# Attention on TensorE: products in groups of 32 output rows, a merged add on GpSimd, and an own end for the last head pair

## The reference

```python
x = x + conv_attention(group_norm(x))        # x: (16, 192, 32, 32) float32, 32 groups
# for each of the 16 images, N = 1024 pixels, 6 heads of 32 channels:
qkv  = xhat.T @ qkv_w.T                       # (N, 576)
attn = softmax(q @ k.T * 32**-0.5)            # (6, N, N)
out  = (attn @ v).reshape(N, 192) @ proj_w.T + proj_b
```

## Time and profile before

| | us |
|---|---|
| median of 3 runs | 1589.49 (1588.39 to 1589.64) |
| the profiled execution | 1588.74 |
| its span, first to last instruction | 1586.9 |
| TensorE busy | 1494.0 (94%), 8800 passes and 8800 weight loads |
| GpSimd busy | 1318.7 (83%) |
| ScalarE busy | 1197.4 (75%) |
| VectorE busy | 1165.1 (73%) |

### The profile page before, as it was taken

The page is one execution under the profiler, slowest core; times in us unless marked ns, Lnnn a source line. Parts: engine busy times, 40 slices in busy tenths (PEclk is TensorE's granted clock), DMA queues, the critical chain, the costliest instruction groups (busy, mean ns, idle before and its releaser), DMA issues.

```text
span 1586.9 us, 24547 instructions
## 1 busy us (share of the span) xinstructions
PE 1494.0 (94%) x8800; PEld 515.2 (32%) x8800; DVE 1165.1 (73%) x2022; ACT 1197.4 (75%) x2001; POOL 1318.7 (83%) x645
## 2 busy tenths in 40 slices
PE   3799999999999999999999999999999999999972
PEld 1233333333333333333333333333333333333220
DVE  4887877887787788778778877877887787877600
ACT  2277887978788797878879787887978787776850
POOL 4168988989899898989989898998989898888980
PEclk9799999999999999999999999999999999999995
DMA  3422161604325161522526152252515033241112
GB/s 102 80 38 65 42 108 36 120 23 104 58 61 108 50 105 37 100 49 65 104 54 104 44 93 45 71 99 54 108 42 93 17 82 61 55 83 39 35 48 60
DMA packets 86106, 108.87 MB, mean 69 GB/s; under 512 B 38240, under 2 KB 50912, under 8 KB 85984
## 3 DMA queue, kind: packets, MB, share of 16 engines
q1 hardware_dynamic: 85984, 107.30, 32.5%
HBM read 42.98 MB, written 13.15 MB: 35 GB/s over the span
## 4 chain that ended last, share of the span: by engine, by line
PE 68%; ACT 9%; DMA 8%; POOL 5%; SPq 4%; DVE 3%; issue 3%; POOLq 0%; DVEq 0%; ACTq 0%
PE heads_ps L615 17%; PE max_ps L524 16%; PE scores_ps L600 15%; PE extra_ps L574 6%; DMA sums_spread<-sums_sb 6%; ACT probs L729 5%; PE extra_ps L583 3%; POOL prob_pairs L793 3%; SPq L416 2%; PE extra_ps L587 2%; PE extra_ps L588 2%; PE extra_ps L585 2%; PE extra_ps L584 2%; POOL prob_pairs L799 1%; ACT xhat_a_hi L692 1%
## 5 line engine op out<-in xcount | busy, mean ns | idle before, releaser
L892 DVE TENSOR_REDUCE half_max<-max_ps 128x1 f32<-128x512 f32 x1536 | 984.3, 684 | 283.2 <-PE max_ps L524 272.8
L729 ACT ACTIVATE probs<-scores_ps,exp_scale 128x512 f32<-128x512 f32 x1536 | 974.7, 698 | 283.8 <-PE scores_ps L600 273.7
L793 POOL TENSOR_TENSOR prob_pairs<-probs 128x1024 f32<-128x1024 f32 x384 | 896.1, 2358 | 164.6 <-ACT probs L729 164.0
L524 PE MATMUL max_ps<-k_stack,q_stack 96*128 96x512 f16 x1536 | 588.7, 384 | 9.6 <-DVE half_max L892 4.8
L600 PE MATMUL scores_ps<-q_stack,k_stack 98*128 98x512 f16 x1536 | 582.5, 381 | 9.3 <-ACT probs L729 7.5
L615 PE MATMUL heads_ps<-probs,v_sb 128*32 128x512 f32 x3072 | 410.0, 606 | 1.7 <-ACT probs L729 0.8
L524 PEld LDWEIGHTS max_ps<-k_stack,q_stack 96*128 96x128 f16 x1536 | 150.4, 98 | 279.9 <-issue 105.9
L799 POOL TENSOR_TENSOR prob_pairs<-prob_pairs 128x1024 f32<-128x1024 f32 x96 | 224.1, 2355 | 0.0
L600 PEld LDWEIGHTS scores_ps<-q_stack,k_stack 98*128 98x128 f16 x1536 | 150.3, 98 | 180.1 <-ACT probs L729 39.6
L574 PE MATMUL extra_ps<-prob_pairs,ones 128*32 128x512 f32 x1152 | 134.3, 599 | 5.8 <-POOL prob_pairs L793 5.8
L615 PEld LDWEIGHTS heads_ps<-probs,v_sb 128*32 128x32 f32 x3072 | 61.0, 108 | 151.7 <-issue 130.2
(11 more groups left out here) (118 smaller groups left out, 926.1 us busy)
## 6 DMA issues: line engine op xcount, KB each, us to landing
q_stack<-qk_hi SPq DMA_DIRECT2D x96, 128.0 KB, 4.2
k_stack<-qk_hi SPq DMA_DIRECT2D x96, 128.0 KB, 5.7
inv_sb<-inv_rows SPq DMA_DIRECT2D x48, 256.0 KB
x_res<-x SPq DMA_DIRECT2D x16, 768.0 KB, 5.4
out<-x_res SPq DMA_DIRECT2D x16, 768.0 KB, 4.9
x_sb<-x SPq DMA_DIRECT2D x16, 512.0 KB, 6.6
x_sb<-x SPq DMA_DIRECT2D x32, 256.0 KB, 7.9
q_stack<-qk_lo SPq DMA_DIRECT2D x48, 128.0 KB, 4.4
```

What stands on the lines that cost most here:

```text
L524: pe.matmul(max_ps[:, bank, :], q_stack[0:STACK, par, h, P * tile:P * (tile + 1)], k_stack[0:STACK, par, h, HALF * half:HALF * (half + 1)] ...
L729: nc.scalar.activation(probs[:, a, s % RING, HALF * half:HALF * (half + 1)], scores_ps[:, u_bank(s, u), :], ACT.Exp, scale=exp_scale[:, 0: ...
L793: nc.gpsimd.tensor_tensor(prob_pairs[:, a, q, :], probs[:, a, (s - 1) % RING, :], probs[:, a, s % RING, :], ALU.add).then_inc(pairs_added, 1)
L892: nc.vector.tensor_reduce(half_max[:, a, tile, half:half + 1], max_ps[:, bank, :], AX_X, ALU.max).then_inc(max_read[bank], 1)
```

## The change

Every f16 product in the loop is issued in groups of 32 output rows, each with its own weight load of 32 columns and its own strip of 32 partitions in PSUM, so that it has the form that the weighing and the sums have. The four (or three) groups stream the same moving operand. GpSimd's adds take both heads of a pair in one operation of 2 x 1024 columns. The sums' 24 passes are split over units 2 and 3. The last pair of the last batch leaves the shared path: GpSimd stops after its first sum of four, TensorE sums the last four slots straight from `probs`, VectorE takes the reciprocal over 512 columns in PSUM and divides, the projections go to seven free banks with the third pair's part read from where it lies, and four stores replace one.

```diff
-ADDED = (2, 4, 8, 10)
-READY = (2, 6, 8, 10)
+ADDED = (1, 2, 4, 5)
+READY = (1, 3, 4, 5)
@@ tensor
+            def in_groups(to, weights, moving, start, stop):
+                for at in range(0, weights.shape[-1], D):
+                    last = pe.matmul(to[at:at + D, :], weights[:, at:at + D], moving, start=start, stop=stop)
+                return last
...
-                pe.matmul(max_ps[:, bank, :], q_stack[0:STACK, par, h, P * tile:P * (tile + 1)],
+                in_groups(max_ps[:, bank, :], q_stack[0:STACK, par, h, P * tile:P * (tile + 1)],
                           k_stack[0:STACK, par, h, HALF * half:HALF * (half + 1)],
-                          start=True, stop=True).then_inc(max_filled[bank], 1)
+                          True, True).then_inc(max_filled[bank], 1)
...
-                elif kind == "sums" and part == 0:
-                    pe.wait_ge(pairs_added, READY[-1] * (PAIRS * st.summed(i) + i + 1))
-                    for q in range(QUAD_AT, PAIRS_A_HEAD):
+                elif kind == "sums":
+                    if part == 0:
+                        pe.wait_ge(pairs_added, READY[-1] * (PAIRS * st.summed(i) + i + 1))
+                    for q in ((QUAD_AT,), range(QUAD_AT + 1, PAIRS_A_HEAD))[part]:
...
-            run_steps(step)
+            extras = run_steps(step)
+            pe.wait_ge(extra_freed, extras)
+            pe.wait_ge(pairs_added, READY[-1] * LAST + READY[QUAD_AT])
+            for n in range(RING + 1):
+                for half in range(HALVES):
+                    for a in range(2):
+                        at, cols = D * (2 * half + a), slice(HALF * half, HALF * (half + 1))
+                        summed = prob_pairs[:, a, QUAD_AT, cols] if n == 0 else probs[:, a, n - 1, cols]
+                        last = pe.matmul(extra_ps[at:at + D, :], ones[:, 0:D], summed, start=(n == 0), stop=(n == RING))
+            last.then_inc(extra_filled, 1)
...
+            pe.wait_ge(attn_moved, MOVE * ATTN_MOVES * LAST)
+            for i in range(QUARTERS):
+                product(0, last_bank(i), wp_hi[:, :, o], wp_lo[:, :, o], attn_a_hi[:, n], attn_a_lo[:, n], None)
+            pe.wait_ge(heads_hi_ready, LAST + 1)
+            pe.wait_ge(heads_lo_ready, LAST + 1)
+            for i in range(QUARTERS):
+                pe.matmul(last_bank(i), wp_hi[rows, 1, o], heads_hi[rows, :], start=False, stop=False)
+                pe.matmul(last_bank(i), wp_lo[rows, 1, o], heads_hi[rows, :], start=False, stop=False)
+                pe.matmul(last_bank(i), wp_hi[rows, 1, o], heads_lo[rows, :], start=False,
+                          stop=True).then_inc(last_projected, 1)
@@ gpsimd
-                        for a in range(2):
-                            pool.wait_ge(probs_ready, SCORE_UNITS * (SLOTS * st.b + s) + 2 * (a + 1))
-                            nc.gpsimd.tensor_tensor(prob_pairs[:, a, q, :],
-                                                    probs[:, a, (s - 1) % RING, :],
-                                                    probs[:, a, s % RING, :], ALU.add).then_inc(pairs_added, 1)
+                        pool.wait_ge(probs_ready, SCORE_UNITS * (SLOTS * st.b + s + 1))
+                        nc.gpsimd.tensor_tensor(prob_pairs[:, :, q, :], probs[:, :, (s - 1) % RING, :],
+                                                probs[:, :, s % RING, :], ALU.add).then_inc(pairs_added, 1)
...
@@ vector
+            nc.vector.reciprocal(inv_sb[:, :], extra_ps[:, :]).then_inc(inverted, 1)
+            nc.vector.tensor_tensor(heads_out[:, :], heads_ps[:, :], inv_sb[:, :], ALU.mult).then_inc(divided, 1)
+            nc.vector.tensor_tensor(heads_lo[:, :], heads_out[:, :], heads_hi[:, :],
+                                    ALU.subtract).then_inc(heads_lo_ready, 1)
```

More of the change, by code:

```diff
@@ L115 @@
 ATTN_MOVES = 4
+LAST = PAIRS * BATCH - 1
+QUARTERS = 4
 STACK_MOVES = 6
@@ L186, in due @@
             return [(self.b, self.parity, at // every)]
-        if at % every == 0 and -SLOTS <= at < 0 and self.tail:
+        if at % every == 0 and -SLOTS <= at < 0 and self.tail and not (self.closing and at == -every):
             return [(self.b - 1, 1 - self.parity, (at + SLOTS) // every)]
@@ L205, in run_steps @@
         extras = st.ordinal(SLOTS)
+    return extras
 def due(count):
@@ L491, in step @@
                         load_x(b + 4)
-                    if s == SLOTS - 1 and st.tail:
+                    if s == SLOTS - 1 and st.tail and not st.closing:
                         sp.wait_ge(extra_freed, st.ordinal(PROJ_SLOTS[-1]) + 1)
@@ L497, in _ @@
             run_steps(step)
-            sp.wait_ge(y_stored, MOVE * (BATCH + 1))
+            for i in range(QUARTERS):
+                t, half = divmod(i, 2)
+                n = slice(HALF * half, HALF * (half + 1))
+                sp.wait_ge(y_ready, i + 1)
+                sp.dma_start(out[BATCH - 1, OM * t:OM * (t + 1), n], x_res[:, t, n]).then_inc(y_stored, MOVE)
+            sp.wait_ge(y_stored, MOVE * (BATCH + QUARTERS))
         @block.tensor
@@ L552, in fill @@
                     to = extra_ps[:, C * part:C * (part + 1)]
[L553 to L557, removed]
+                    in_groups(to, xhat_a_hi[:, par, n], w_hi[:, 0, o], True, False)
+                    in_groups(to, xhat_a_hi[:, par, n], w_lo[:, 0, o], False, False)
+                    in_groups(to, xhat_a_lo[:, par, n], w_hi[:, 0, o], False, False)
+                    in_groups(to, xhat_b[:, par, n], w_hi[:, 1, o], False, False)
+                    second = in_groups(to, xhat_b[:, par, n], w_lo[:, 1, o], False, True)
                     last = second if part == 1 else None
@@ L576, in fill @@
                                                  start=(q == QUAD_AT), stop=(q == PAIRS_A_HEAD - 1))
+                    last = last if part == 1 else None
                 if last is not None:
@@ L956, in step @@
                                                 AX_X, ALU.max, negate=True).then_inc(neg_max_ready, 1)
-            run_steps(step)
+            extras = run_steps(step)
+            dve.wait_ge(divided, LAST)
+            dve.wait_ge(extra_filled, extras + 1)
+            nc.vector.reciprocal(inv_sb[:, :], extra_ps[:, :]).then_inc(inverted, 1)
+            dve.wait_ge(heads_done, TILES * (LAST + 1))
+            dve.wait_ge(heads_lo_ready, LAST)
+            dve.wait_ge(inverted, LAST + 1)
+            nc.vector.tensor_tensor(heads_out[:, :], heads_ps[:, :], inv_sb[:, :], ALU.mult).then_inc(divided, 1)
+            dve.wait_ge(attn_moved, MOVE * ATTN_MOVES * LAST)
+            dve.wait_ge(heads_hi_ready, LAST + 1)
+            nc.vector.tensor_tensor(heads_lo[:, :], heads_out[:, :], heads_hi[:, :],
+                                    ALU.subtract).then_inc(heads_lo_ready, 1)
+            dve.wait_ge(res_biased, 2 * BATCH)
+            for i in range(QUARTERS):
+                t, half = divmod(i, 2)
+                n = slice(HALF * half, HALF * (half + 1))
+                dve.wait_ge(last_projected, i + 1)
+                nc.vector.scalar_tensor_tensor(out=x_res[:, t, n], in0=last_bank(i), scalar=proj_unscale[0:OM, 0:1],
+                                               in1=x_res[:, t, n], op0=ALU.mult, op1=ALU.add).then_inc(y_ready, 1)
 def u_bank(s, u):
```

50 lines of the change are left out of this document (31 added, 19 removed).

## The result

The changed kernel takes 1623.54 us (median of 4, 1619.11 to 1630.68) for 1588.94 before (median of 4, the three of the table ahead and one more): ratio 1.0222, 95% interval 1.0183 to 1.0261, so slower by 2.2%. The forecast was 1504.

What follows compares the result with a forecast made beforehand. TensorE was taken to set the pace, ScalarE just behind in B and C, GpSimd in D and F. Body -61, last batch -1, end -24 made -86 us: 1503 from 1588.74 profiled, 1504 as median; range 1482 to 1590.

Steps and rivals of the forecast that it cites:

- The switches, 0.23 us a weighing: TensorE around each weighing: changing between wide and 32-row products loses 0.23 us; the groups remove it except beside transposes.
- Four groups in the time of one, value groups too: TensorE's f16 products: four groups take 0.22 us as one pass did; a value group 0.025 more, nothing on the path.
- GpSimd's merged add, 4.53 us: GpSimd's add of both heads in one operation takes 4.53 us, for 4.67 as two, and starts when the slot is over.
- What is late next is ScalarE: Slots 8, 16 and 0: ScalarE's first exponential waits for GpSimd's late adds, no earlier than 14.72 us in B, D, F.
- the ring's deadline: Slots 8, 16 and 0 overwrite the ring's slots 4 and 5 of each pair, so must wait for GpSimd's work on them.
- the work of 14.72 us: GpSimd from the start of slot 4, 12 or 20: three adds of 4.53 and a split of the heads of 1.13.
- D and F: Two of a batch's six four-slot stretches, A to F; D starts at slot 12, F at 20; GpSimd is full in both.
- The rival of the late start: B, D and F: GpSimd's late start is not absorbed, each becomes 14.72 us, total 1549; chance 0.12.
- 1.4 us of lateness costs TensorE nothing: At the start of a slot, TensorE's three score banks absorb 1.4 us of ScalarE's lateness if ScalarE catches up afterwards.
- B and C, -1.2: Second and third four-slot stretches of a batch: together 1.2 us shorter, down to 29.9, limited by GpSimd and ScalarE.
- The end, T + 25.4: After the last exponential, T: the span ends 25.4 us later for 49.5, a gain of 24.
- The slow sequencer: TensorE everywhere: its sequencer cannot keep up with 44,040 instructions, 1850 us at 42 ns each; chance 0.2 slower.

Runs made afterwards that it cites:

- the fastest kernel: The changed kernel with an add for each head, later moves of the second and third pair, and the third pair's stack DMAs two slots later: 1502.64 us, ratio 0.9449.

## Why the prediction was wrong, point by point

- **The switches, 0.23 us a weighing: right.** Gone in the changed kernel. The transposes kept theirs, as said: in slot 13 of the kernel with an add for each head, a transpose starts 0.96 after its weighing and the next pass 0.21 later, 1.17 for the 1.20 of before (0.09 + 0.99 + 0.12).
- **Four groups in the time of one, value groups too: right,** and the 0.025 set aside for a value group was not needed.
- **GpSimd's merged add, 4.53 us: right** (4.56 measured), and its start when the slot is over was right too.
- **"What is late next is ScalarE": the step that failed.** The prediction followed the late adds to the ring's deadline and stopped. It had counted the split of the heads among the work of 14.72 us, but did not ask who waits for the split. That is SyncE, whose queue holds four moves for it and, behind them, the shifts that the next pair's first score needs. In this queue the split ends 4.5 us before the fourth operation of the 14.72, but four issues of 0.6, that of the shifts and a landing of 1.7 or more follow it: with the prediction's prices for the adds and the split some 15 us from the first add, and 15.8 in the place shown, where D and F had 14.1 and 13.7. The rival of the late start had the right cause and the wrong price: it gave +1.75 in B, D and F together and 1549, where the cost on top of the groups and the end is 95.7, and 62 of these went with one slot in SyncE's order.
- **"1.4 us of lateness costs TensorE nothing": right for the ring, as far as the runs tell, and beside the point.** The three score banks can absorb ScalarE's lateness; the shifts are an operand of TensorE itself, where nothing absorbs. With the moves out of the way, the merge makes F of batch 8 longer by 1.67 (up to the bound of 14.72), and A, D and E give 0.67, 0.55 and 0.89 back. What is left is C, longer by 1.74. C and F with the merged add, and with an add for each head:

```profile
838.93:856.70 17.77, 16.17 (x276) 6.45 (x264) 13.75 (x23) 15.20 (x27) 15.11 (x6) 1.00 0.93 169
885.77:900.41 14.64, 14.64 (x210) 6.17 (x206) 14.09 (x29) 10.04 (x17) 14.56 (x5) 1.00 0.11 28
```

```profile
824.98:841.01 16.03, 15.61 (x276) 6.59 (x264) 12.89 (x22) 15.19 (x26) 15.80 (x9) 1.00 0.91 164
871.52:884.49 12.97, 12.97 (x190) 5.36 (x186) 12.43 (x26) 9.97 (x17) 12.97 (x7) 1.00 0.06 13
```

- **The wait in slot 11** was missing as well: the late add of slot 9 also holds the division, and ScalarE waits for that in the middle of a slot. That slot is in C, and it is 6.5 us long with the merged add and the later moves, 4.8 with an add for each head.
- **B and C, -1.2: wrong by its full size.** They take 31.1 without the merge, as before. The forecast took ScalarE's busy time as what the stretch could shrink to. B was at ScalarE's pace already: it is busy for 14.3 of 14.65 us with and without the groups. In C, slot 10 gave 0.75 us, and slot 11 took it back: in batch 8 of the fastest kernel it has 5.24 us for 4.21, with 0.90 in which ScalarE waits for the division. This is read from the timelines and was not tried.
- **The end, T + 25.4: right.** It took 1617.3 - 1592.81 = 24.5. The last exponentials and the reciprocal, in the timeline after:

```profile
1589.66 3.15 ACT L781 ACTIVATE probs<-scores_ps,exp_scale 128x512 f32<-128x512 f32 x5 [0.50 <-PE scores_ps L530]
...
1598.36 3.36 DVE L1013 RECIPROCAL inv_sb<-extra_ps 128x512 f32<-128x512 f32 x1 [7.53 <-PE extra_ps L672]
```

  The reciprocal took 3.36 for 3.2. The projections began at T + 14, later than the T + 10.5 forecast; the moves were issued at T + 7 to 9, behind the residual's load, and it was not tried whether that load held them up. TensorE started them 0.43 apart and from 1609.7 on 0.22 apart, back at the full clock, and made up for it.
- **The slow sequencer**, the largest rival at 0.2, was priced from the densest row before, which was only the densest that the work had asked for. The result is on that rival's side, slower, for a reason that is not its own.

## What to carry to other kernels

When an edit makes one operation start later, follow everything behind it in its queue, and behind each waiter in that one's queue, until a transfer or an operand of the bound engine turns up; the deadline that is easiest to see (a ring, a buffer) need not be the one that binds. A merged operation that has to wait for its second half can cost far more than its fixed cost gives back, here 0.1 us an add saved, and 60 to 96 us lost (34 once the moves were out of the way). Products of one form throughout take a switch's cost out of every slot, and the queues that had just enough slack at the old pace are then the next thing to reorder.

## What the runs showed of the hardware

- Changing between TensorE products of 128 and of 32 output rows cost 0.23 us per pair of changes here; changing between f16 and f32 at 32 rows cost nothing. Four f16 products of 32 rows in four strips took the time of one of 128 rows, down to 192 columns (0.08 us for the four with their loads, 20 ns a product in the mean). By the Trainium skill ("TensorE: Matmul & The Clock Gate", Wait — 56ns, not 53.3ns?) starts never come closer than some 25 ns; the products in four strips do here. The loss of fast weight load that "TensorEngine Tiling (Array Packing)" names in its Restrictions and Gotchas cost no time in any stretch shown.
- TensorE took 20 passes and 20 loads, each in groups of four, at 0.082 us for four and four: 10 ns an instruction.
- After a wait of some 2.5 us the granted clock was at half in the following stretch (0.51), and groups that take 0.22 came 0.43 apart.
- VectorE's reciprocal takes 6.6 ns a column over 512 columns (3.36 us), about in line with 5.7 from the two narrow ones.
